# Graph network kernel: key rows loaded to four partitions and spread to all 128 by a shuffle on VectorE

## What is computed

```python
msg = gate * h[dst] * (cw * mj)[:, None]                    # first and third network, once each
agg = jax.ops.segment_sum(msg, src, num_segments=N)
...
for i in range(L):                                          # first network, L = 4 layers
    qi, kj = Q[src], K[dst]
    score = (qi * kj).sum(-1) + 0.1 * (edge_attr * qi[:, :RBF]).sum(-1) + logm[dst]
    smax = jax.ops.segment_max(score, src, num_segments=N)
    es = jnp.exp(jnp.minimum(score - smax[src], 20.0))
    alpha = es / (jax.ops.segment_sum(es, src, num_segments=N)[src] + 1e-10)
    aggi = jax.ops.segment_sum(alpha[:, None] * (h[dst] @ Wm[i]), src, num_segments=N)
...
agg = jax.ops.segment_sum(x[src], dst, num_segments=n)      # second network, twice; fourth, once
```

## Time and profile before

| | us |
|---|---|
| median of the two runs | 19,482.16 |
| profiled execution | 19,526.43 |
| its span on the core | 19,524.7 |
| PE / DVE / ACT / POOL busy | 12,999.4 / 13,101.2 / 6,431.0 / 5,777.7 |
| mean granted TensorE clock | 0.674 of full |
| DMA | 3473.94 MB in 4,204,769 packets, mean 178 GB/s |

### The profile page before, as it was taken

One profiled execution on the slowest core, in us unless ns is written; L12 is line 12 of the kernel. 1 busy time (PEld: TensorE's weight loads), 2 busy tenths in 40 slices (PEclk: granted clock), 3 DMA queues, 4 the chain that ended last, 5 costly groups with the idle time before them and its releaser, 6 DMA issues. The chain is left out here.

```text
span 19524.7 us, 646880 instructions
## 1 busy us (share of the span) xinstructions
PE 12999.4 (67%) x202700; PEld 11041.5 (57%) x202701; DVE 13101.2 (67%) x28429; ACT 6431.0 (33%) x18271; POOL 5777.7 (30%) x5353
## 2 busy tenths in 40 slices
PE   2999995264457667576776667676675457665566
PEld 1777775253346557555665556565574356655556
DVE  4777776458865876468764786647866575747867
ACT  0333330130024456344553446444463202031020
POOL 1888883402201223012320223202231041602205
PEclk9999999975567555765558655595555556585565
DMA  8222226388857667476666767486674466669966
GB/s 317 58 58 58 58 58 55 87 261 216 215 172 241 167 184 234 163 219 167 196 190 220 197 167 213 138 279 171 166 226 145 143 191 195 196 210 254 251 201 179
DMA packets 4204769, 3473.94 MB, mean 178 GB/s; under 512 B 2500900, under 2 KB 3577014, under 8 KB 4204590
## 3 DMA queue, kind: packets, MB, share of 16 engines
q1 hardware_dynamic: 3201726, 1787.26, 35.4%
q0 software_dynamic: 364096, 862.51, 15.9%
q10 hardware_dynamic: 638768, 821.84, 11.7%
HBM read 2323.73 MB, written 1144.88 MB: 178 GB/s over the span
## 5 line engine op out<-in xcount | busy, mean ns | idle before, releaser
L1023 PE MATMUL ps<-arena 128*128 x56160 | 3053.3, 212 | 1831.6 <-DVE arena L1453 1146.1
L637 POOL DMA_INDIRECT arena<-chunk_keys,idx_stage x1820 | 1797.1, 987 | 7895.9 <-DVE arena L1526 2833.7
L1023 PEld LDWEIGHTS ps<-arena 128*128 128x128 bf16 x56160 | 2696.3, 106 | 2189.0 <-issue 2059.1
L1453 DVE TENSOR_SCALAR arena<-arena,iota_row 128x1024 bf16<-128x1024 uint8 x2600 | 1956.7, 755 | 2446.6 <-PE ps L1023 1741.0
L1059 PE MATMUL ps<-arena 128*128 128x49 bf16 x56160 | 2669.7, 216 | 880.0 <-DVE arena L1472 695.7
L1059 PEld LDWEIGHTS ps<-arena 128*128 128x128 fp8e4 x56160 | 2423.6, 118 | 1021.5 <-issue 984.0
L1044 PE MATMUL ps<-arena 128*128 x37440 | 1931.6, 209 | 1246.7 <-DVE arena L1453 714.4
L765 ACT ACTIVATE arena<-ps 128x392 f32<-128x392 f32 (+1 forms) x3900 | 1711.7, 481 | 2836.3 <-PE ps L1023 1535.9
L1044 PEld LDWEIGHTS ps<-arena 128*128 128x128 bf16 x37440 | 1670.2, 113 | 1571.1 <-issue 1499.2
L612 POOL DMA_INDIRECT edge_records<-arena x1600 | 2016.4, 1260 | 487.4 <-issue 465.2
L793 ACT ACTIVATE arena<-arena,neg_big 128x1024 bf16<-128x1024 bf16 x1040 | 1193.0, 1148 | 1142.0 <-DVE node_max L1552 1134.2
(11 more groups left out here) (275 smaller groups left out, 18305.9 us busy)
## 6 DMA issues: line engine op xcount, KB each, us to landing
arena<-node_hot_a SPq DMA_DIRECT2D x2340, 256.0 KB
chunk_keys<-arena ACTq DMA_DIRECT2D x1820, 196.0 KB, 4.0
chunk_rows<-arena ACTq DMA_DIRECT2D x1040, 196.0 KB, 4.4
arena<-key_rows_b SPq DMA_DIRECT2D x1560, 128.0 KB, 4.3
arena<-edge_hot_a SPq DMA_DIRECT2D x1560, 128.0 KB
chunk_gated<-arena ACTq DMA_DIRECT2D x520, 324.0 KB, 4.4
arena<-edge_records SPq DMA_DIRECT2D x1040, 160.0 KB
arena<-key_rows_a SPq DMA_DIRECT2D x1040, 128.0 KB, 3.9
```

The costliest lines, as they stand in the source:

```text
L637: pool.indirect_dma_start(out=arena[:, scratch_at + o * w:scratch_at + (o + 1) * w], out_offset=None, in_=tab, in_offset=bass.IndirectOffs ...
L1023: last = pe.matmul(psv[:, 2 * r + j // tpb, (j % tpb) * w:(j % tpb + 1) * w], ht4[:, s, j * P:(j + 1) * P], tab_d[:, bass.ds(b * (3 * 2 * ...
L1453: dve.tensor_scalar(ht4[:, s, :], kb4[:, s, :], iop[:, 0:1], None, ALU.is_equal).then_inc(ht_made, 1)
```

## The change

`load_rows` writes 1 KB to each of the partitions 0, 32, 64 and 96 in place of all 128. A new step of VectorE, `row_spread`, copies the row of the first partition of each group of 32 to all of the group by a `stream_shuffle` on 256 float32 words, in place. The compare of a strip now waits for the shuffle of it and stands one turn later in VectorE's lists: lag 1 in place of lag 0. The keys are recoded once, so that four bytes together always are a normal float32 number: 0 to 125 becomes 1 to 126, 126 and 127 become 129 and 130, a hole 131; the two iota tables that they are compared with are recoded alike.

```diff
@@ SP @@
                 def step(k, s):
                     hold(sp, "sp", (ht_made, hm_no * NS + k - 3))
-                    sp.dma_start(kb4[:, s % 4, :], row.rearrange("(s j) c -> s (j c)", j=C8)[bass.ds(k, 1), :].squeeze(0).partition_broadcast(P)).then_inc(kb_loaded[s % 4], 16)
+                    sp.dma_start(kb4[0:P:32, s % 4, :], row.rearrange("(s j) c -> s (j c)", j=C8)[bass.ds(k, 1), :].squeeze(0).partition_broadcast(4)).then_inc(kb_loaded[s % 4], 16)
@@ VectorE, once @@
+            def coded(dst, src, rest):
+                do(dve.tensor_scalar(rest, src, float(P - 2), 0.5, ALU.is_ge, ALU.add))
+                do(dve.tensor_scalar(dst, src, float(P), None, ALU.min))
+                do(dve.scalar_tensor_tensor(dst, rest, 2.0, dst, ALU.mult, ALU.add))
...
-            do(dve.tensor_copy(key_s, kl[:, :, 0]))
+            coded(key_s, kl[:, :, 0], key_d)
+            coded(ioc[:, :], ioc[:, :], junk[:, 0:P])
+            coded(iop[:, :], iop[:, :], junk[:, 0:1])
...
-            do(dve.tensor_copy(key_d, kd_g))
+            coded(key_d, kd_g, rows.bitcast(BF16)[:, 0:NT])
+            do(dve.memset(kb.bitcast(F32), 0.0))
@@ VectorE, every pass with key rows @@
+            def row_spread(hm_no):
+                def step(k, s, *_):
+                    s = s % 4
+                    hold(dve, "dve", (kb_loaded[s], landed(hm_no, k, s, 4)))
+                    dve.stream_shuffle(kb4f[:, s, :], kb4f[:, s, :], [0] * 32).then_inc(kb_spread, 1)
+                return step
+
             def hot_turned(hm_no, kbp_no, kept=None):
                 def step(k, s, *_):
                     s = s % 4
-                    dve.wait_ge(kb_loaded[s], landed(hm_no, k, s, 4))
+                    dve.wait_ge(kb_spread, hm_no * NS + k + 1)
...
-                walk(nc, dve, NS, [(0, hot_turned(hm_no, kbp_no)), *more])
+                walk(nc, dve, NS, [(0, row_spread(hm_no)), (1, hot_turned(hm_no, kbp_no)), *more])
...
-                    steps = [(0, hot_turned(HM_G1 + 1, kbp_no, ht_stored)), (4, add_up(hs_no, 6)), (1, logit), (1, message), (2, first)]
+                    steps = [(0, row_spread(HM_G1 + 1)), (1, hot_turned(HM_G1 + 1, kbp_no, ht_stored)), (4, add_up(hs_no, 6)), (1, logit), (1, message), (2, first)]
```

More of the change, by code:

```diff
@@ L314, in build @@
         kb4 = kb.rearrange("p (s c) -> p s c", s=4)
+        kb4f = kb.bitcast(F32).rearrange("p (s c) -> p s c", s=4)
         ht4 = hot_t.rearrange("p (s c) -> p s c", s=4)
@@ L371, in build @@
         kb_loaded = [sem(f"kb_loaded{s}") for s in range(4)]
+        kb_spread = sem("kb_spread")
         ht_made, ht_used = sem("hot_t_made"), sem("hot_t_used")
```

## The result

The changed kernel takes 20,241.11 us, the median of two runs (20,232.47 and 20,249.74), against 19,482.16: a ratio of 1.039 with a 95% interval of 1.0345 to 1.0434, 759 us more. Its profiled execution spans 20,248.0 us, 723 more than before. The forecast was 20,070 us, slower because of the gated pass. The gated pass is slower, but a second loss of nearly its size, in C1, stood in the sum as nothing, and most other terms are off in size.

A forecast was written before the change was run, and what follows sets the result against it. Load loops were taken to bound the gated pass, store landing the layers. 920 - 312 - 73 + 47 + 0 + 10 = +592 us gave 20,118 for the profiled execution, 20,070 us as median; range 19,400 to 20,750.

The forecast's parts named there:

- The lag in the gated pass: Gated pass: VectorE stands still 2.42 us from compare to TensorE's `sc_done` before its add-up; pass +920 us.
- the load loop closes harder still: 5.14 + L, with L = 3.3 that is 8.44: Gated pass: key-load loop holds one strip instead of two, 8.44 us per strip with landing L, above VectorE's 7.1.
- The landing time: Small key load, issue to landing (L): 3.0 us in spread passes, 3.3 in the gated pass.
- its own signs: Prediction falls if VectorE does not idle before the gated pass's add-up, or if key rows land in 2 us.
- It loses 0.4 to 0.5 of landing and gets 0.42 of shuffle: 0: Pass C1: one load loop over two strips (6.5 us), no net change; -127 us at small L (2.0).
- the second case: Rival: small load quick, L = 2.0 everywhere; gated pass +583, sum -158 us, 19,325 us; chance 0.25.
- Spreads: Spread passes: layers -312 us, G1 and G2 -73, C2 and C3 +47; load loop at least 1.50 us per strip.
- (3.5 + 1.2)/3: Layers' spreads: store landing 3.5 us plus 1.2 for issues and evacuation, over three periods: 1.57 us per strip, -312 us.
- The shuffle: VectorE's new copy of key rows: 0.42 us each, upper bound 1.22, nothing if fully hidden.
- Coding of the keys: Recoding once, four more passes over 2080 elements and a memset, VectorE alone: +10 us.
- Case 3: Rival: over 2% faster, TensorE's clock staying high in the gated pass; pass +364, all -377 us; chance 0.07.
- Case 4: Rival: shuffle slow at 1.2 us, VectorE needing 1.95 us per strip in spreads; +1763 us, 21,240 us; chance 0.08.

The follow-up runs named there:

- the two serial kernels: Changed kernel with lag 0 everywhere, and the kernel before, each issuing a strip's load only after the previous strip's compare: 23,459.35 and 24,950.08 us.
- The kernel with C1's loss taken away: Changed kernel with the compare back at lag 0 in pass C1 alone, lag 1 kept elsewhere: 20,551.81 us.

## Why the prediction was right, step by step

- *The lag in the gated pass, mechanism.* Right. VectorE idles 2.58 us (2.42 forecast) ahead of `add_up` in every strip of the stretch read. The lag alone makes the loss, its removal takes it away, and turning TensorE's two steps round halves it.
- *The same, size.* The step "the load loop closes harder still: 5.14 + L, with L = 3.3 that is 8.44" is wrong. L is about 2.05, which brings that loop to 7.2; VectorE's own loop (7.1 forecast) decides, at 7.34: 4.37 of work as forecast, 2.58 of waiting for 2.42, and 0.4 of gaps for 0.3. VectorE waited for a key row only 8 times. +632 us for +920; for L = 2.0 the prediction itself had +583. The small load had been priced by subtracting too little from the wide one: 0.5 to 1 us, where the two serial kernels differ by 1.1 to 1.2.
- *The landing time.* The Trainium skill, "DMA: Bandwidth & Descriptors" (Anatomy of one DMA), gives some 2.0 us of fixed cost. Its heading is for transfers that GpSimd issues in software; these are SyncE's, on a queue that the page of the profile calls hardware_dynamic. The runs come near it all the same: 2.05 in C1, about 1.8 with little beside it. It was weighed in the prediction, and the rows' higher guess was taken instead. By its own signs the prediction "falls" if key rows land in 2 us. They do, so what it built on the slower load has fallen; its other sign, VectorE's idle time ahead of `add_up`, held.
- *C1: "It loses 0.4 to 0.5 of landing and gets 0.42 of shuffle: 0".* This is the step that failed. The sum counted the load's loop, and not what the lag does to VectorE's second step there. The order shown for the gated pass has its twin in C1: compare of k-1, TensorE, evacuation, copy of keys k, `hot_edges` k. It makes +547 us for 0: the lag costs 631 (1388 against 757 with lag 0), and the rest of the change gives back 84. The order of all these lists stood in the program; the prediction followed it through the other engines in the gated pass and not in C1. With this term at +547 and L at 2.0 the sum of the second case, -158 us, would have been +516 (C1's -127 replaced).
- *Spreads.* Forecast -312 (layers), -73 (G1, G2), +47 (C2, C3), measured -190, -150, -112. With L near 2 the load loop of these passes comes to about 1.2 us, not 1.50, and G1, G2, C2 and C3 gained more than forecast (1.34 and 1.20 us per strip). The layers gained less, 1.67 for 1.57. The step "(3.5 + 1.2)/3" had the stores still setting the pace, but they land in 2.1 us and ScalarE waits for them no longer; what holds the layers is TensorE's pause at its loop's head (0.2 per strip) and, close behind, ScalarE's 1.6 (read from its waits).
- *The shuffle.* 0.442 us for 0.42 forecast. The Trainium skill, "VectorE: DVE Perf Modes" (the perf-mode tier table), has it in the basic mode alone, one element per cycle, and the row fits that; runs with one length cannot show a rate.
- *Coding of the keys.* The first compare of G1 comes at 3812.0 us, where it came at 3803.6: 8 us for 10.
- *Rivals.* Case 2 (0.25) had the load right and the time wrong, since C1 was missing. Case 3 is out: the gated pass was granted 0.50 of the clock, as before. Case 4 is out: the shuffle takes 0.442 us and not 1.2.

The errors of the gated pass (-288) and of the spreads (-114) partly cancelled that of C1 (+547), so the 171 us between forecast and result look smaller than the misses in it. That the time came out slower by over 2% is luck: the terms that the prediction did work out measure 176 us together (723 - 547), 0.9%, and that is the second case's "within 2%". The kernel with C1's loss taken away shows it: 20,551.81 us for 20,436.21, 1.006.

## What to carry to other kernels

When a step gets a lag of one turn, go through every pass that uses it, and in each write down the step that now follows it directly on its engine; if that step needs, through other engines' lists, something that was released by the lagged one, the whole round trip turns into a stall on every turn. Here the lag was meant to hide 0.2 us between shuffle and compare; it made waits of 2.6 and 3.1 us, and 2.5 and 2.4 us more per strip, in two of ten passes. The idea itself, a smaller load for a broadcast and the copy on a half-idle engine, was worth 3%, and the kernel that keeps it without the lag takes 0.971 of the time before.

## What was not expected of the hardware

In the profiles of the two kernels with serial loads the row of the granted TensorE clock cannot be taken at its word. The clock row of the one with the small load, over 40 slices of the run, reads full speed for three quarters of it:

```profile
PEclk9999999999999999999999999999999555555555
```

The same picks L1025 of that kernel in G1 and in G2, which pick the same amount (busy us and count of PE and of PEld, PEclk, DMA share, GB/s), and in the changed kernel's G1:

```profile
3804.00:4701.00 897.00, 501.12 (x6210) 441.40 (x6211) 1.00 0.25 96
20113.00:21025.00 912.00, 500.92 (x6212) 441.64 (x6213) 0.50 0.24 95
```

```profile
3812.00:4160.00 348.00, 276.39 (x6143) 251.35 (x6144) 1.00 0.63 244
```

A matmul takes 81 ns in G1 at a reading of 1.00 and 81 ns in G2 at 0.50 (1.2 GHz), and in the changed kernel 45 ns at 1.00 (2.4 GHz). So in the first stretch of the serial kernel TensorE very probably ran at the lower level, and the 1.00 is not a grant: the trace of that kernel has its first record of the clock at 18,173.7 us, where the row falls, and none before. A clock row should be read together with the length of one instruction at it. No result above uses the clock of these two kernels.

The wide broadcast load delayed other queues' stores much more than its bytes: it was 128 of 520 KB per strip in a layer, and with 4 KB in its place the stores landed in 2.1 us in place of 4.4. Whether its packets or its bytes do that is open, as said.
